# Expert bounds in registers and two gather buffers in an attention and mixture-of-experts kernel

## Chip, core and metric

The program runs on one core of one Trainium2 chip. The metric is the device time of one execution in microseconds (us). TensorE does the matmuls, VectorE, ScalarE and GpSimd the elementwise work; SyncE, ScalarE and GpSimd issue DMAs. Each engine has a sequencer of its own, which also does register arithmetic, branches and loads of values into registers.

## What is computed

A transformer block on x of 2 x 1024 tokens and 512 features: layer norm, causal attention with 16 heads in 4 groups, a shared two-layer MLP, and 32 experts of which each token uses 6. The part the change concerns:

```python
idx, w = _route(xf, Wr, br)                 # 6 of 32 experts a token
gate = jnp.zeros((T, E), w.dtype).at[jnp.arange(T)[:, None], idx].add(w)
def step(acc, ew):
    w1, w2, g = ew                          # 256 x 512 and 512 x 256
    h = jnp.square(jax.nn.relu(xf @ w1.T)) @ w2.T
    return (acc + g[:, None] * h, None)
acc, _ = jax.lax.scan(step, jnp.zeros_like(xf), (W1, W2, gate.T))
...
x = x + attention(xn) + shared(xn) + acc
```

## The kernel before

The kernel has three stages. The first (to about 190 us) normalises, routes, runs the shared MLP and builds a list of tokens sorted by expert, cut into tiles of 128 rows. The second (190 to 611 us) runs the experts over these tiles. The third does attention and adds the experts' rows, gathered by token, to the output.

Precision is kept by splitting every fp32 operand into an upper and a lower fp32r part, so each product is three matmuls (upper by upper, upper by lower, lower by upper).

**The expert stage.** The number of tiles of an expert depends on the data. `place_rows` on VectorE writes the first tile of each expert to `first_pair` in SBUF (`pairs` are tiles there); every expert has at least two. `pair_bound` (L355) loads one entry into a register of the engine that asks. `over_experts` loops over 8 rounds (`es`) of 4 experts (`s` in `SLOTS`, each with its own weight slot) and calls the engine's body with the bounds `lo` and `hi`. In `over_experts` of before, a round loads its first `lo`, and each expert loads its `hi`. Each body does tile `lo` outside of the inner loop, with the pieces of weight work of that expert around it, and the others in a loop over `lo + 1` to `hi`.

Five engines run the same loops side by side, tied by semaphores only:

- SyncE (`store_tiles`): for each expert it issues the load of the weights three experts ahead (`eraw <- we`, 1 MB, L442), then per tile the store of the tile's output rows (`expert_outputs <- ysb`, L451). The bounds of an expert are read before its weight load.
- GpSimd: one flat loop over all tiles. For tile p it waits until `mx_ready` tells that buffer p % XG is free, compares p % XG with each slot number, and in the slot that fits copies the tile's row numbers (L598), runs the small operation `settle` (L390), and starts the gather of 128 rows of normalised tokens into `xg[:, slot]` (L601, an indirect DMA, queue 0).
- TensorE (`expert_tiles`): `hidden_tile(p)` does 12 matmuls with the first weights (L800, L801, L804), and then, again by comparing (p + 1) % XG with each slot number (L807), `transpose_gathered` of the gathered rows of tile p + 1, four transposes (L792), after a wait for `xg_in` of that slot. They free the buffer: the last one adds to `mx_ready`. `output_tile(p - 1)` follows, six matmuls with the second weights (L815, L816, L819), then `transpose_hidden(p)`, two transposes (L828) that need `mhsq`.
- ScalarE (`expert_uppers`): per tile `mrelu`, `xgT_hi`, the copy of the output to `ysb`, and `hT_hi`; per expert four pieces of upper weight parts (L1086) two experts ahead.
- VectorE (`expert_lowers`): per tile `mhsq`, `xgT_lo`, `hT_lo`; per expert four pieces of lower weight parts (`w_lo`, L1210).

XG is 4, so a gather may start once the transposes of the tile four before are done. What is named `xg` holds 128 x 512 fp32 per buffer. The order of the work around the change is that in which the code is written; no planner moves it.

Of the kernel before, what the change touches and what calls it, by code (L numbers as in the profile page):

```python
# [8 lines left out]
I32 = mybir.dt.int32  # L9
# [4 lines left out]
P = 128  # L14
# [6 lines left out]
E, M = 32, 256  # L21
# [19 lines left out]
COMB = 3  # L41
MINT = T * TOPK // P
MAXT = MINT + 2 * E
XG = 4
YB = 4
WP = 4
NCOMB = TOPK * NT // GROUPS
# [68 lines left out]
def moe_attention_kernel(nc, x, wa, we, wr, br, out):  # L116
# [10 lines left out]
    with ExitStack() as ctx:  # L127
        def sb(name, shape, dt, stack=ctx):
            return stack.enter_context(nc.sbuf_tensor(name, shape, dt))
# [12 lines left out]
        y_rows = sb("y_rows", [P, TILES, 8], I32)  # L142
        y_gate = sb("y_gate", [P, TILES, TOPK], F32)
        tok_idx = sb("tok_idx", [P, MAXT + 1], I32)
        first_pair = sb("first_pair", [P, 2, E + 1], I32)
        comb_idx = sb("comb_idx", [P, NCOMB], I32)
        comb = sb("comb", [P, COMB, D], F32)
        araw = sb("araw", [P, 2, PIECE], F32)
# [204 lines left out]
        def pair_bound(eng, e, row=0):  # L353

            return eng.value_load(first_pair[0:1, row, bass.ds(e, 1)], min_val=0, max_val=MAXT + row)  # L355
# [14 lines left out]

            return slice(c * (W_COLS // WP), (c + 1) * (W_COLS // WP))

        def over_experts(eng, body, row=0):

            with eng.Fori(0, E // SLOTS) as es:
                lo = pair_bound(eng, es * SLOTS, row)
                for s in range(SLOTS):
                    hi = pair_bound(eng, es * SLOTS + s + 1, row)
                    body(es * SLOTS + s, s, lo, hi, es)
                    lo = hi  # L380

        def attend_groups(eng, attend, turn):
            attend(FIRST, turn * GROUPS)
# [11 lines left out]
        def _(sp):  # L395
# [43 lines left out]
            def store_tiles(e, s, lo, hi, es):  # L439

                sp.wait_ge(ew_lo, (e + (NSH + 2)) * WP)
                sp.dma_start(eraw[:, (s + AHEAD) % 2, :],  # L442
                             we[bass.ds((e + AHEAD) * P, P), :]).then_inc(eraw_in[(s + AHEAD) % 2], 16)
                with sp.Fori(lo, hi) as p:

                    for half in range(2):
                        with sp.If(p % 2 == half):
                            sp.wait_ge(y_stored[half], past((p // 2) * 16))
                            sp.sem_inc(y_free, 1)
                            sp.wait_ge(y_copied, past(p + 1))  # L450
                            sp.dma_start(y_d[bass.ds(p * P, P), :],  # L451
                                         ysb[:, bass.ds(p % YB, 1), :].rearrange("p s d -> p (s d)")
                                         ).then_inc(y_stored[half], 16)

            over_experts(sp, store_tiles)

# [174 lines left out]
        def _(pe):  # L631
# [163 lines left out]
            def hidden_tile(p, s):  # L795

                w_hi, w_lo = w1(hi_slot(s)), w1(lo_slot(s))
                pe.wait_ge(mx_hi, p + 1)
                for k in range(KD):
                    pe.matmul(ps_h, xgT_hi[:, k, :], w_hi[:, k, :], start=(k == 0), stop=False)  # L800
                    pe.matmul(ps_h, xgT_hi[:, k, :], w_lo[:, k, :], start=False, stop=False)  # L801
                pe.wait_ge(mx_lo, p + 1)
                for k in range(KD):
                    mm = pe.matmul(ps_h, xgT_lo[:, k, :], w_hi[:, k, :], start=False, stop=(k == KD - 1))  # L804
                mm.then_inc(mh_ready, 1)
                for slot in range(XG):
                    with pe.If((p + 1) % XG == slot):  # L807
                        transpose_gathered(slot, p + 1)
# [13 lines left out]
            def transpose_hidden(p, weights=None):  # L822
                pe.wait_ge(mhsq_ready, past(p + 1))
                for m in range(KM):
                    if m and weights is not None:

                        pe.wait_ge(ew_lo, weights)
                    mm = pe.transpose(ps_g[:, m * P:(m + 1) * P], mhsq[:, m * P:(m + 1) * P], ident[:, :])  # L828
                mm.then_inc(mt_ready, 1)
# [6 lines left out]
            def expert_tiles(e, s, lo, hi, es):  # L836

                pe.wait_ge(ew_lo, (e + NSH) * WP + 2)
                hidden_tile(lo, s)
                if s:  # L840
                    output_tile(lo - 1, s - 1)
                else:
                    with pe.If(es > 0):
                        output_tile(lo - 1, SLOTS - 1)
                transpose_hidden(lo, (e + (NSH + 1)) * WP)
                with pe.Fori(lo + 1, hi) as p:
                    hidden_tile(p, s)
                    output_tile(p - 1, s)
                    transpose_hidden(p)

            over_experts(pe, expert_tiles)
            output_tile(pair_bound(pe, E) - 1, SLOTS - 1)
# [104 lines left out]
        def _(act):  # L957
# [160 lines left out]
            def expert_uppers(e, s, lo, hi, es):  # L1118

                arrived, slot = e // 2 + (NSH // 2 + 2), (s + 2) % SLOTS  # L1120
                relu_hidden(lo)
                upper_tokens(lo + 1)
                upper_weights(0, slot, arrived)
                if s:
                    copy_output(lo - 1)
                else:
                    with act.If(es > 0):
                        copy_output(lo - 1)
                upper_hidden(lo)
                upper_weights(1, slot, arrived)  # L1130
                with act.Fori(lo + 1, hi) as p:
                    relu_hidden(p)
                    upper_tokens(p + 1)
                    copy_output(p - 1)
                    upper_hidden(p)
                upper_weights(2, slot, arrived)
                upper_weights(3, slot, arrived)

            over_experts(act, expert_uppers)
            copy_output(pair_bound(act, E) - 1)  # L1140
# [64 lines left out]
        def _(dve):  # L1205
# [112 lines left out]
            def place_rows():  # L1318

                dve.wait_ge(ranks_ready, 1)  # L1320
                for h in range(2):
                    dve.wait_ge(xn_out[h], 16 * B)
                dve.wait_ge(xnT_ready, B * NT)
                chain(dve.tensor_scalar(pairs_f, ps_total, float(P - 1), None, ALU.add))
                chain(dve.tensor_copy(pairs_i[:, :], pairs_f))
                chain(dve.tensor_scalar(pairs_i[:, :], pairs_i[:, :], 7, None, ALU.logical_shift_right))
                chain(dve.tensor_copy(pairs_f, pairs_i[:, :]))
                chain(dve.tensor_scalar(pairs_f, pairs_f, 2.0, None, ALU.max))
                chain(dve.tensor_tensor_scan(scan_f, scan_ones[:, :], pairs_f, 0.0, ALU.mult, ALU.add))
                chain(dve.memset(first_pair[:, :, 0:1], 0))  # L1330
                for row in range(2):
                    chain(dve.tensor_copy(first_pair[:, row, 1:E + 1], scan_f))
                dve.tensor_scalar(first_pair[:, 1, E:E + 1], scan_f[:, E - 1:E], 1.0, None, ALU.add).then_inc(pairs_ready, 1)
                dve.wait_ge(pairs_ready, 1)

                chain(dve.tensor_tensor(row_base, scan_f, pairs_f, ALU.subtract))
                chain(dve.tensor_scalar(row_base, row_base, float(P), 1.0, ALU.mult, ALU.add))
                chain(dve.tensor_tensor(rrow, ps_rank[:, :].rearrange("p (t e) -> p t e", t=TILES),
                                        row_base.unsqueeze(1).to_broadcast([P, TILES, E]), ALU.add))
                chain(dve.tensor_tensor(rrow, rrow, rsel[:, :, :].bitcast(F32), ALU.mult))  # L1340
                hold()
                for t in range(TILES):
                    last = dve.max(out=top_y[:, t, :], in_=rrow[:, t, :])
                chain(last)
                dve.tensor_scalar(y_rows[:, :, :], top_y[:, :, :], -1.0, None, ALU.add).then_inc(y_rows_ready, 1)
                dve.wait_ge(y_rows_ready, 1)
                chain(dve.tensor_scalar(part_i[:, 0, :, :], y_rows[:, :, :], P - 1, None, ALU.bitwise_and))
                chain(dve.tensor_scalar(part_i[:, 1, :, :], y_rows[:, :, :], 7, None, ALU.logical_shift_right))
                chain(dve.tensor_copy(part_f[:, :, :, :], part_i[:, :, :, :]))
# [111 lines left out]
            def expert_lowers(e, s, lo, hi, es):  # L1461
                slot = (s + 2) % SLOTS
                square_hidden(lo)
                lower_tokens(lo + 1)
                lower_weights(e + 2, 0, slot)
                lower_hidden(lo)
                lower_weights(e + 2, 1, slot)
                with dve.Fori(lo + 1, hi) as p:
                    square_hidden(p)
                    lower_tokens(p + 1)  # L1470
                    lower_hidden(p)
                lower_weights(e + 2, 2, slot)
                lower_weights(e + 2, 3, slot)

            over_experts(dve, expert_lowers)

# [111 lines left out]
```

## Time and profile before

| | us |
|---|---|
| median of 3 runs (1704.72 to 1709.8) | 1704.78 |
| the profiled execution | 1705.53 |
| its span, first to last instruction | 1703.8 |
| of the span: first stage with the change over to the experts | 206 |
| expert stage from its third tile on, 206 to 611 | 405 |
| attention and the rest | 1093 |

The span is what the profile's views divide up; the profiled execution is 1.7 us longer than it. Busy TensorE in the views means that its pipeline holds a matmul, and a granted clock of 1.00 is 2.4 GHz, 0.50 is 1.2 GHz. Register, branch and load-to-register instructions are not counted as busy; they show under the queue of their engine (PEldq, DVEq, ACTq, SPq) in the view of a source line. "issue" as a releaser is idle time that ends with nothing the profile shows.

### The profile page before, as it was taken

Reading aid. Unit: us, or ns where it says so; the run is one execution under the profiler, and the core shown is the slowest. Engines: PE = TensorE matmul, PEld = TensorE weight load, DVE = VectorE, ACT = ScalarE, POOL = GpSimd, SP = SyncE. Lnnn points to the kernel's source line nnn. Section 1 sums busy time; section 2 is a strip of 40 time slices with the busy share of each in tenths; the row PEclk is TensorE's granted clock in tenths of the full one; section 3 lists DMA queues with packets and bytes.
Section 4 is the critical chain, followed back from the end, with each engine's and each line's share of the span. In section 5 each row is a group of like instructions: output and inputs, shape, how many; then the busy total and the mean of one; then the engine's idle time right before and its main releaser. Section 6 shows DMA issues by size and latency. Waiting matters only on the chain.

```text
span 1703.8 us, 31632 instructions
## 1 busy us (share of the span) xinstructions
PE 1580.1 (93%) x8812; PEld 1349.1 (79%) x8813; DVE 1174.4 (69%) x2277; ACT 823.0 (48%) x1687; POOL 355.6 (21%) x590
## 2 busy tenths in 40 slices
PE   6886899999999969999999999995999999999996
PEld 5765688888888857888888888874788888888885
DVE  5679665565666545866866876872795785785785
ACT  3410266666666643544544544542454453453453
POOL 3541433333333310011011011020101101101101
PEclk9988799999999989999999999997999999999999
DMA  5850466666676640111111110214101201201102
GB/s 199 315 229 1 136 215 217 226 217 222 209 234 212 218 160 32 32 56 51 31 55 50 31 55 25 93 45 143 44 20 56 62 19 56 62 19 56 38 7 81
DMA packets 61736, 180.15 MB, mean 106 GB/s; under 512 B 6736, under 2 KB 6864, under 8 KB 56912
## 3 DMA queue, kind: packets, MB, share of 16 engines
q1 hardware_dynamic: 36800, 107.84, 18.3%
q0 software_dynamic: 16640, 54.54, 11.5%
q10 hardware_dynamic: 8208, 16.78, 2.6%
q8 instruction: 34, 0.56, 0.1%
q14 instruction: 54, 0.44, 0.1%
HBM read 122.77 MB, written 56.36 MB: 105 GB/s over the span
## 4 chain that ended last, share of the span: by engine, by line
PE 86%; DVE 7%; issue 3%; ACT 1%; DMA 1%; DVEq 0%; ACTq 0%; POOLq 0%; SPq 0%
PE bank L638 8%; PE bank L640 8%; PE bank L639 8%; PE bank L919 7%; PE ps_s L638 5%; PE ps_s L640 5%; PE ps_s L639 5%; PE ps_s L907 4%; PE ps_s L902 4%; PE ps_s L908 4%; PE ps_s L800 4%; PE ps_s L804 3%; PE ps_s L801 3%; PE ps_s L815 3%; PE ps_s L819 3%
## 5 line engine op out<-in xcount | busy, mean ns | idle before, releaser
L1180 ACT ACTIVATE probs<-ps_s,negmax 128x128 f32<-128x128 f32 (+7 forms) x256 | 189.6, 741 | 187.2 <-DVE negmax L1506 186.1
L1210 DVE TENSOR_TENSOR pT_lo<-bank,pT_hi 128x512 fp32r<-128x512 f32 x288 | 196.5, 687 | 76.4 <-ACT pT_hi L1188 75.0
L1188 ACT ACTIVATE pT_hi<-bank 128x512 fp32r<-128x512 f32 x288 | 169.1, 597 | 149.7 <-PE bank L919 148.4
L390 POOL TENSOR_TENSOR settled<-ident 128x1 f32<-128x1 f32 x192 | 54.7, 285 | 774.1 <-DVE acc L1533 764.4
L1506 DVE TENSOR_REDUCE negmax<-ps_s 128x1 f32<-128x128 f32 (+7 forms) x256 | 189.2, 751 | 21.6 <-issue 9.8
L638 PE MATMUL ps_s<-xT_hi,wa_hi 128*128 128x512 f32 x384 | 156.3, 407 | 26.5 <-DVE wa_lo L1210 26.5
L919 PE MATMUL bank<-ident,probs 128*128 128x128 f32 x1152 | 167.4, 272 | 2.0 <-DVE pT_lo L1210 2.0
L919 PEld LDWEIGHTS bank<-ident,probs 128*128 128x128 f32 x1152 | 139.5, 141 | 29.8 <-DVE pT_lo L1210 2.4
L640 PE MATMUL ps_s<-xT_hi,wa_lo 128*128 128x512 f32 x384 | 153.1, 399 | 0.0
L639 PE MATMUL ps_s<-xT_lo,wa_hi 128*128 128x512 f32 x384 | 152.5, 397 | 0.0
L902 PE MATMUL ps_s<-kT_hi,qT_hi 128*128 128x512 f32 (+3 forms) x384 | 140.2, 365 | 8.3 <-ACT probs L1180 5.4
L907 PE MATMUL ps_s<-kT_lo,qT_hi 128*128 128x512 f32 (+3 forms) x384 | 142.4, 371 | 0.0
L800 PE MATMUL ps_s<-w_hi,xgT_hi 128*128 128x256 f32 x444 | 121.8, 307 | 21.7 <-issue 16.6
L1513 DVE TENSOR_SCALAR probs<-probs,rnorm 128x128 f32<-128x128 f32 (+7 forms) x256 | 133.3, 521 | 9.1
L908 PE MATMUL ps_s<-kT_hi,qT_lo 128*128 128x512 f32 (+3 forms) x384 | 132.8, 346 | 0.0
L638 PE MATMUL bank<-pT_hi,v_hi 128*128 128x512 f32 x288 | 125.0, 434 | 3.1 <-DVE cT_lo L1210 3.1
L601 POOL DMA_INDIRECT xg<-normed_tokens,comb_idx x112 | 115.7, 1033 | 24.1 <-issue 20.4
L1210 DVE TENSOR_TENSOR hT_lo<-ps_s,hT_hi 128x256 fp32r<-128x256 f32 x111 | 47.1, 424 | 96.9 <-ACT hT_hi L1096 66.8
L640 PE MATMUL bank<-pT_hi,v_lo 128*128 128x512 f32 x288 | 113.6, 394 | 0.0
L639 PE MATMUL bank<-pT_lo,v_hi 128*128 128x512 f32 x288 | 112.8, 392 | 0.0
L801 PE MATMUL ps_s<-w_lo,xgT_hi 128*128 128x256 f32 x444 | 111.9, 284 | 0.0
L800 PEld LDWEIGHTS ps_s<-w_hi,xgT_hi 128*128 128x128 f32 x444 | 84.9, 191 | 30.2 <-issue 29.3
(188 smaller groups left out, 3740.1 us busy)
## 6 DMA issues: line engine op xcount, KB each, us to landing
eraw<-we SPq DMA_DIRECT2D x37, 1024.0 KB
expert_outputs<-ysb SPq DMA_DIRECT2D x111, 256.0 KB
araw<-wa SPq DMA_DIRECT2D x40, 512.0 KB, 3.9
expert_outputs<-comb ACTq DMA_DIRECT2D x1, 16384.0 KB, 52.5
normed_tokens<-xn SPq DMA_DIRECT2D x4, 1024.0 KB, 6.7
out<-acc SPq DMA_DIRECT2D x2, 2048.0 KB, 7.8
res<-x SPq DMA_DIRECT2D x2, 1024.0 KB, 6.6
acc<-x SPq DMA_DIRECT2D x2, 1024.0 KB, 14.0
```

The source lines that it names most:

```text
L638: pe.matmul(out_, lh, rh, start=(first and k == 0), stop=False)
L639: pe.matmul(out_, lh, rl, start=False, stop=False)
L640: mm = pe.matmul(out_, ll, rh, start=False, stop=(last and k == parts - 1))
L800: pe.matmul(ps_h, xgT_hi[:, k, :], w_hi[:, k, :], start=(k == 0), stop=False)
L902: pe.matmul(o, q_h, kT_hi[:, ks], start=True, stop=False)
L907: pe.matmul(o, q_h, kT_lo[:, ks], start=False, stop=False)
L908: mm = pe.matmul(o, q_l, kT_hi[:, ks], start=False, stop=True)
L919: mm = pe.transpose(ps_t[blk % 2][:, h * P:(h + 1) * P], probs[:, i % 2, h, a * P:(a + 1) * P], ident[:, :])
L1180: act.activation(probs[:, i % 2, a, 0:keys], src, ACT.Exp, bias=negmax[:, i % 2, a:a + 1], accum_out=rowsum[:, i % 2, a:a + 1]).then_inc(e ...
L1188: act.activation(pT_hi[:, blk % RING, :], ps_t[blk % 2][:, :], ACT.Copy).then_inc(pt_hi_ready, 1)
L1210: dve.tensor_tensor(out_, whole, upper.bitcast(F32), ALU.subtract).then_inc(signal, 1)
L1506: dve.tensor_reduce(negmax[:, i % 2, a:a + 1], src, AX.X, ALU.max, negate=True).then_inc(max_ready, 1)
```

## The change

It has three parts. In `over_experts` the first bounds are set before the loop (0, and a load of entry 1), and both are kept in two registers from round to round. Each body now loads the bound of the expert after the next one (`after = pair_bound(..., e + 2)`) at a place of its own and returns it: SyncE behind the weight load, TensorE behind `hidden_tile(lo)`, ScalarE behind `upper_hidden(lo)`, VectorE behind `lower_hidden(lo)`. XG goes from 4 to 2, in the buffers, their semaphores and the comparisons of TensorE and GpSimd. `first_pair` gets one more entry, which is cleared with the others since the last expert's load reads it. The number and the work of the tiles stay.

```diff
-XG = 4
+XG = 2
...
-        first_pair = sb("first_pair", [P, 2, E + 1], I32)
+        first_pair = sb("first_pair", [P, 2, E + 2], I32)
...
-        def over_experts(eng, body, row=0):
+        def over_experts(eng, body):
+            lo_reg = eng.alloc_register()
+            hi_reg = eng.alloc_register()
+            eng.reg_mov(lo_reg, 0)
+            eng.reg_mov(hi_reg, pair_bound(eng, 1))
             with eng.Fori(0, E // SLOTS) as es:
-                lo = pair_bound(eng, es * SLOTS, row)
+                lo = eng.snap(lo_reg, min_val=0, max_val=MAXT)
+                hi = eng.snap(hi_reg, min_val=0, max_val=MAXT)
                 for s in range(SLOTS):
-                    hi = pair_bound(eng, es * SLOTS + s + 1, row)
-                    body(es * SLOTS + s, s, lo, hi, es)
-                    lo = hi
+                    lo, hi = hi, body(es * SLOTS + s, s, lo, hi, es)
+                eng.reg_mov(lo_reg, lo)
+                eng.reg_mov(hi_reg, hi)
...
                              we[bass.ds((e + AHEAD) * P, P), :]).then_inc(eraw_in[(s + AHEAD) % 2], 16)
+                after = pair_bound(sp, e + 2)
                 with sp.Fori(lo, hi) as p:
...
                 hidden_tile(lo, s)
+                after = pair_bound(pe, e + 2)
                 if s:
                     output_tile(lo - 1, s - 1)
...
                 upper_hidden(lo)
+                after = pair_bound(act, e + 2)
                 upper_weights(1, slot, arrived)
...
-                chain(dve.memset(first_pair[:, :, 0:1], 0))
+                chain(dve.memset(first_pair[:, :, :], 0))
...
                 lower_hidden(lo)
+                after = pair_bound(dve, e + 2)
                 lower_weights(e + 2, 1, slot)
```

On TensorE, where one expert ends and the next begins, before: L828 is `transpose_hidden` of the last tile, L846 the inner loop's end, L800 the first matmul of `hidden_tile(lo)`.

```order
L828 MATMUL ps_s<-ident,mhsq 128x128 [waits mhsq_ready]
L828 MATMUL ps_s<-ident,mhsq 128x128
L846 REGISTER_ALU
L846 COMPARE_AND_BRANCH
L355 REGISTER_ALU
L355 TENSOR_LOAD first_pair
L355 ISA x2
L838 REGISTER_ALU
L798 REGISTER_ALU [waits ew_lo]
L800 MATMUL ps_s<-w_hi,xgT_hi 128x256 [waits mx_hi]
```

The same place after (L835, L854 and L807 are the lines just named):

```order
L835 MATMUL ps_s<-ident,mhsq 128x128 [waits mhsq_ready]
L835 MATMUL ps_s<-ident,mhsq 128x128
L854 REGISTER_ALU
L854 COMPARE_AND_BRANCH
L845 REGISTER_ALU
L805 REGISTER_ALU [waits ew_lo]
L807 MATMUL ps_s<-w_hi,xgT_hi 128x256 [waits mx_hi]
```

The load is gone from there. After, it stands in the middle of an expert's first tile, behind the second and last of the slot comparisons (L814) with its transposes (L799) and in front of `output_tile` (L822):

```order
L814 COMPARE_AND_BRANCH
L797 ISA
L799 MATMUL ps_s<-ident,xg 128x128 [waits xg_in1]
L799 MATMUL ps_s<-ident,xg 128x128 x3
L814 UNCONDITIONAL_BRANCH
L355 REGISTER_ALU
L355 TENSOR_LOAD first_pair
L355 ISA x2
L851 COMPARE_AND_BRANCH
L822 MATMUL ps_s<-w_hi,hT_hi 128x512 [waits mhhi_ready]
```

So the load moved behind the wait for `xg_in`, and two of four comparisons are gone. On VectorE, in the first tile of an expert after the change (L1221 is the subtraction that L1210 was, L1451 the square that L1440 was):

```order
L1221 TENSOR_TENSOR hT_lo<-ps_s,hT_hi 128x256 [waits mhhi_ready]
L355 ISA
L355 TENSOR_LOAD first_pair
L355 ISA x2
L1459 REGISTER_ALU
L1221 TENSOR_TENSOR w_lo<-eraw,w_hi 128x512 [waits ew_hi]
L1480 ISA
L1480 UNCONDITIONAL_BRANCH
L1480 ISA
L1451 TENSOR_TENSOR mhsq<-mrelu 128x256 [waits mrelu_ready]
```

Before, VectorE had its load between the last piece of an expert's `w_lo` and the square of the next expert's first tile; now it is between `hT_lo` of the first tile and the second piece of `w_lo`.

## Rows read from the trace of the kernel before

**Rows 1.** The page, first line.

```profile
span 1703.8 us, 31632 instructions
```

**Rows 2.** Windows (start:end length, busy us by engine, clock, DMA share, GB/s).

```profile
190.00:206.00 16.00, 10.50 (x51) 9.35 (x50) 12.93 (x20) 7.02 (x15) 5.15 (x8) 0.68 0.55 204
206.00:611.00 405.00, 387.14 (x2600) 344.07 (x2599) 242.04 (x449) 264.67 (x558) 151.81 (x316) 1.00 0.69 218
```

**Rows 3.** Timeline of TensorE (start us, us, engine line, operation, idle before).

```profile
205.25 0.36 PE L800 MATMUL ps_s<-w_hi,xgT_hi 128*128 128x256 f32 x1
...
248.56 0.36 PE L800 MATMUL ps_s<-w_hi,xgT_hi 128*128 128x256 f32 x1
...
253.62 0.38 PE L800 MATMUL ps_s<-w_hi,xgT_hi 128*128 128x256 f32 x1 [1.33 <-issue]
...
257.11 0.36 PE L800 MATMUL ps_s<-w_hi,xgT_hi 128*128 128x256 f32 x1
...
264.07 0.36 PE L800 MATMUL ps_s<-w_hi,xgT_hi 128*128 128x256 f32 x1
...
267.85 0.38 PE L800 MATMUL ps_s<-w_hi,xgT_hi 128*128 128x256 f32 x1
...
269.38 0.60 PE L792 MATMUL ps_s<-ident,xg 128*128 128x128 f32 x4
...
279.78 0.38 PE L800 MATMUL ps_s<-w_hi,xgT_hi 128*128 128x256 f32 x1 [0.75 <-issue]
...
609.50 0.36 PE L800 MATMUL ps_s<-w_hi,xgT_hi 128*128 128x256 f32 x1
```

**Rows 4.** Waits, 206 to 611 us (us in total, times, longest).

```profile
POOL comb_idx L598 <- PE ps_s L792: 210.6, 105, 3.7
...
PEld ps_s L800 <- issue: 24.6, 31, 1.8
...
PEld ps_s L828 <- DVE mhsq L1440: 2.4, 9, 0.4
```

**Rows 5.** Source line L355 (count, ns min/median/max, first and last start).

```profile
L355 PEldq FUSED_REGOPS  x49: 51/157/171, 188.4 to 613.2; - x49
L355 PEldq TENSOR_LOAD <-first_pair x41: 299/337/1119, 187.9 to 612.6; - x41
...
L355 DVEq TENSOR_LOAD <-first_pair x40: 305/486/1003, 196.4 to 604.2; - x40
```

**Rows 6.** Source line L807, the slot comparisons of TensorE.

```profile
L807 PEldq COMPARE_BRANCH  x444: 66/200/373, 195.5 to 610.5; - x148
```

**Rows 7.** Timeline of VectorE, mhsq of an expert's second and third tile.

```profile
552.66 0.42 DVE L1440 TENSOR_TENSOR mhsq<-mrelu 128x256 f32<-128x256 f32 x1
...
556.02 0.42 DVE L1440 TENSOR_TENSOR mhsq<-mrelu 128x256 f32<-128x256 f32 x1 [0.60 <-ACT mrelu L1092]
```

**Rows 8.** Timeline of SyncE's queue, three of 32 weight loads.

```profile
274.43 0.36 SPq L442 DMA_DIRECT2D eraw<-we  x1
...
374.02 0.36 SPq L442 DMA_DIRECT2D eraw<-we  x1
...
500.50 0.36 SPq L442 DMA_DIRECT2D eraw<-we  x1
```

**Rows 9.** Timeline of GpSimd, two of 112 gathers.

```profile
270.99 0.99 POOL L601 DMA_INDIRECT xg<-normed_tokens,comb_idx  x1 [0.21 <-issue]
...
275.11 0.99 POOL L601 DMA_INDIRECT xg<-normed_tokens,comb_idx  x1 [0.23 <-issue]
```

**Rows 10.** Gather queue, packets in windows 256.88:260.28, 374.59:379.79, 500.80:506.40.

```profile
q0 software_dynamic: 80, 0.26, 31.0%
...
q0 software_dynamic: 73, 0.22, 10.8%
...
q0 software_dynamic: 80, 0.26, 12.7%
```

**Rows 11.** The queue of weights and stores, window 300.96:304.43 (packets, MB, share).

```profile
q1 hardware_dynamic: 203, 1.00, 88.2%
```

More of the change, by code:

```diff
@@ L453, in store_tiles @@
                                          ).then_inc(y_stored[half], 16)
+                return after
             over_experts(sp, store_tiles)
@@ L849, in expert_tiles @@
                     transpose_hidden(p)
+                return after
             over_experts(pe, expert_tiles)
@@ L1137, in expert_uppers @@
                 upper_weights(3, slot, arrived)
+                return after
             over_experts(act, expert_uppers)
@@ L1473, in expert_lowers @@
                 lower_weights(e + 2, 3, slot)
+                return after
             over_experts(dve, expert_lowers)
```

## Prediction, made before the changed kernel ran

> **What bounds the kernel now.** The windows by stage come first [rows 1, 2]. The change touches the expert stage, 206 to 611 us: there TensorE is busy 387 of 405 us at the full clock (1.00), so TensorE's stream of tiles sets the time, and the stages around it stay as they are. TensorE's own timeline shows the pace: two tiles take 6.96 us inside an expert (257.11 to 264.07), 3.48 each, but 3.78 us pass before the tile at 267.85, which opens an expert, and 5.06 us pass before the one at 253.62 (248.56 to 253.62), which also opens a round of four experts [rows 3]. There are 111 tiles (444 comparisons, four each [rows 6]). From the third, 205.25, to the last, 609.50, there are 108 periods, 404.25 us; at 3.48 they would be 375.8. So **28.4 us** are lost at the openings of experts. The waits put 24.6 us of idle before the weights of L800 down to "issue", nothing the profile shows as a releaser [rows 4]. The source view of L355 tells what it is: TENSOR_LOAD of a bound on TensorE's queue, 299/337/1119 ns, followed by register work (157 ns) [rows 5]. One is in front of every expert, two in front of a round.
>
> **Loads of bounds on TensorE.** A load with its register work takes 0.31 + 0.16 us and the steps between, about 0.75 us (a round's second load costs 5.06 - 3.78 = 1.28 us together with the loop's own branch). Inside an expert the sequencer has 0.3 to 0.4 us in hand, so an ordinary border loses 0.3 us, more when the load is slow (up to 1.1), and a round 1.6. After the change nothing of this stands between transpose_hidden of the last tile and hidden_tile of the next. Ordinary borders (24) should show no gap at all; at the 7 rounds the two register moves and the loop's branch remain, and I leave 0.3 us each, 2 us. Of the 28.4 some 3 us are not in front of L800 but in the middle of a tile, before L828 (2.4 us at waits for mhsq [rows 4]): VectorE's own load sits before square_hidden(lo) and makes mhsq late. **Removed: 28.4 - 3 - 2 = 23 us.** Bounds: 20 and 26.
>
> **The same loads in their new places.** TensorE: the sequencer reaches the load about 0.9 us after the tile's start (it is held until xgT_lo is there, then passes two comparisons of 0.2 us [rows 6]), is through at 1.65, and output_tile's first weights are due at 1.87. Hidden, cover 0.2 us, as long as nothing holds the sequencer before it. VectorE: the load follows lower_hidden(lo) and precedes weight piece 1. Now mhsq of an expert's second tile starts 552.66, right behind that piece; undisturbed it would come 3.48 before the next one, 556.02, so at 552.54 [rows 7]. With at least 0.31 us of load and as much register work as TensorE's, the piece and mhsq come about 0.35 later still, 0.45 in all, and TensorE bears 0.35 (the hand of the sequencer above): some 0.1 us an expert, 3 us, and the 3 us of today's late mhsq go. Zero net; bounds -3 and +8 (VectorE's load has a median of 486 ns [rows 5]). ScalarE: its load stands behind upper_hidden(lo) while copy_output still runs on the engine, and its queue is served in order behind that; nothing, bound 2 us. SyncE: the weight load eraw leaves before the bound is read, so some 0.7 us earlier by the same sum (274.43 [rows 8] would be 273.7); the store behind it waits for ysb anyway. A page of the Trainium skill (DMA: Bandwidth & Descriptors, section Latency and other measured facts) gives tensor_load a floor of about 600 ns. The rows show 299 on TensorE, so here the floor does not hold; by it VectorE's piece would come 0.3 us later in 32 experts and the sum would rise by up to 9 us.
>
> **Four comparisons to two.** TensorE's cost 200 ns each [rows 6] but run while matmuls stream; worth nothing in steady state. On GpSimd the gather of slot 0 leaves 3.14 us after its tile's start (270.99 against 267.85) [rows 3, 9], each further slot one comparison later, near 0.15; slots 2 and 3 vanish. Nothing on the path by itself.
>
> **Two gather buffers instead of four** is the expensive part. GpSimd waits for TensorE's transposes in every tile already (210.6 us, 105 times [rows 4]): it fills a buffer the moment it is free. The gather for tile p may start when the transposes of p - 4 are done; now of p - 2. Those stand in tile p - 3, the gather leaves 3.14 to 3.3 us into that tile, and its rows are read by L792 some 1.5 us into tile p - 1 (269.38 against 267.85 [rows 3]). The time it has is 2 x 3.48 + 1.5 - 3.2 = **5.2 us**, where it had 12.2. How long does it take? The one issued at 256.88, with no weight load near, had its 80 packets by 3.4 us [rows 10]. Gathers issued within a microsecond behind a weight load are slow: that of 374.59, 0.57 us behind the load of 374.02, had 73 of 80 by 5.2 us; that of 500.80, 0.3 us behind, had all 80 only by 5.6 [rows 8, 10]. The weight load and its neighbours keep the DMA engines 88% busy and move 1.00 MB in 3.5 us [rows 11]; a gather behind all of it would need 3.4 + 3.5 = 6.9. So one gather in each expert (31 of them) overruns: by 0.3 us at the low end, by 1.7 at the high end, and I take 1.1 for the pattern of today. The earlier eraw shifts the pair apart by 0.7 us, of which I credit 0.2: 0.9 x 31 = **28 us**.
>
> **The new place of the load makes that worse.** The weight load leaves 6.6 us after its expert's first tile began (274.43 less 267.85 [rows 3, 8]), after the change near 5.9 or less, in the second tile; the gather it hits is the second tile's (275.11 [rows 9]), which after the change is for three tiles on, so that its transposes stand in the fourth tile. In an expert of three tiles (267.85 to 279.78 [rows 3]; I count 19 of 32 experts that way) the fourth is the next expert's first, where the bound is loaded right behind the transposes. TensorE's sequencer is then held at xg_in, and comparison plus load (0.2 + 0.75 us) start only when the rows land, against 0.44 us of transposes (four at 0.11) that cover them: 0.45 us on top, 19 x 0.45 = **8.5 us**.
>
> **Sum.** -23 + 0 + 28 + 8.5 = +13.5. Span 1703.8 + 13.5 = 1717.3; the profiled execution took 1705.5, 1.7 more than its span, and the median of the runs is 1704.78, 0.75 below it: 1718.3 for a median. **Forecast 1718 us**, slower.
>
> **Rivals.** (1) *Turn-taking hides the gather.* If DMA engines alternate between the gather's queue and the weights' queue, a gather's four 4 KB packets an engine (64 of its 80, over 16) wait for four weight packets at most, 8 of which an engine moves in 3.5 us, 0.43 each: 3.4 + 1.7 = 5.1 us, just within 5.2. Then no transposes wait, only the 23 us count, and the time is 1682, 1 to 8 us more with stragglers. That is the other side, and it decides at 5.2 us. Against it stand the 73 of 80 packets at exactly that point, and the 80 of 500.80 only at 5.6. The Trainium skill has the rule (DMA: Bandwidth & Descriptors, section Queues, rings and completion order): each engine round-robins between its queues, packet by packet. By that rule, these traces disagree. (2) *Balance.* With eraw 0.7 us earlier and the gather up to 0.3 earlier, the second may meet only the tail of the first. At 0.5 us an overrun, 15 us, and 5 for the loads behind: 1702, no difference. For it: 500.80, 0.3 us behind its weight load, overran by only 0.4. Against: 374.59 and 275.11 sit 0.57 and 0.68 us behind theirs, and that is where most sit today. (3) *Worse.* Overruns at 1.7 and 0.5 more in the short experts, 62 us less 23, to 1744; and long pauses can cost the clock: it stood at 0.68 in 190 to 206, where TensorE was busy 10.5 of 16 us, while the gaps of up to 1.8 us in the expert stage never moved it from 1.00 [rows 2, 4]. Stalls of 2 to 3 us lie between. (4) *The registers do not hold the bounds* and the loads stay: nothing supports it, the order shows the loads moved.
>
> **Chances.** Forecast with its spread (1708 to 1733) 0.64; balance (1700 to 1710) 0.15; turn-taking and anything else under 1700, 0.12; worse than 1733, 0.09. The likeliest case gives the time. To hold 8 in 10 the range takes the forecast's spread and the balance: 1701 to 1733. About 0.3% (5 us) is what a measurement of this kernel can tell from no change: faster 0.12, same 0.16, slower 0.72.
>
> **What the profile after would show.** Right: no idle "issue" over 0.1 us before the first expert matmul at ordinary borders; TENSOR_LOAD on TensorE mostly near 300 ns, since it no longer falls 3 to 4 us behind eraw; a new wait of TensorE's transposes for the DMA of xg, about one an expert, near 1 us, 25 to 40 us in all; more idle before output_tile in first tiles of experts than elsewhere; GpSimd's wait for ps_s unchanged in kind. Wrong: if the waits for xg sum to less than 15 us, the overruns are mis-sized; if output_tile waits for nothing in first tiles, the last 8.5 us are wrong; if TensorE pauses before L828 in second tiles by more than 0.2 us, VectorE's load was underrated; if the granted clock drops below 1.00 in the expert stage, the third rival holds.

## The result, and the profile after

| | before | after |
|---|---|---|
| median of 4 runs each, us | 1705.9 | 1731.08 (1728.39 to 1737.47) |
| span of the profiled execution | 1703.8 | 1728.0 |
| third tile to last tile on TensorE, 108 periods | 404.25 | 428.51 |

The changed kernel takes 1.0146 of the time before (95% interval 1.0121 to 1.017): 25 us slower, where 13 were forecast. All of it lies in the expert stage, as the last row shows. Of the kernels below, the one with SyncE alone changed had one execution of four at a granted clock of 0.58 (2528.93 us), which is left out of its median. The page, the windows (as [rows 2]; the third is one of five short stretches at half clock) and TensorE's timeline (as [rows 3]):

```profile
span 1728.0 us, 31078 instructions
```

```profile
190.00:206.00 16.00, 10.48 (x49) 9.19 (x48) 13.06 (x20) 7.05 (x14) 3.61 (x7) 0.68 0.53 205
206.00:637.00 431.00, 398.44 (x2611) 351.93 (x2610) 238.77 (x451) 261.43 (x560) 156.19 (x322) 0.98 0.64 207
350.50:353.90 3.40, 3.40 (x16) 3.10 (x15) 1.75 (x4) 1.51 (x4) 0.99 (x1) 0.50 0.39 124
```

```profile
205.43 0.38 PE L807 MATMUL ps_s<-w_hi,xgT_hi 128*128 128x256 f32 x1
...
309.65 0.38 PE L807 MATMUL ps_s<-w_hi,xgT_hi 128*128 128x256 f32 x1
...
310.70 0.64 PE L811 MATMUL ps_s<-w_hi,xgT_lo 128*128 128x256 f32 x4
313.16 0.66 PE L799 MATMUL ps_s<-ident,xg 128*128 128x128 f32 x4 [1.82 <-DMA xg<-normed_tokens,comb_idx]
314.31 0.49 PE L822 MATMUL ps_s<-w_hi,hT_hi 128*128 128x512 f32 x1 [0.49 <-issue]
...
315.93 0.36 PE L807 MATMUL ps_s<-w_hi,xgT_hi 128*128 128x256 f32 x1
...
633.94 0.37 PE L807 MATMUL ps_s<-w_hi,xgT_hi 128*128 128x256 f32 x1
```

The tile at 309.65 opens an expert and takes 6.28 us instead of 3.48. Its border is clean, but the transposes (L799) wait 1.82 us for the gathered rows, and then output_tile (L822) waits another 0.49 us, because TensorE's sequencer had been held at the same wait and reached the bound load only afterwards. The waits of after, 206 to 637 us (as [rows 4]), and the loads of bounds (as [rows 5]):

```profile
POOL comb_idx L605 <- PE ps_s L799: 238.5, 107, 4.2
...
PEld ps_s L799 <- DMA xg<-normed_tokens,comb_idx: 31.7, 21, 2.3
...
PEld ps_s L822 <- issue: 8.8, 16, 1.0
...
PEld ps_s L835 <- DVE mhsq L1451: 3.0, 13, 0.2
...
PEld ps_s L807 <- issue: 0.2, 1, 0.2
```

```profile
L355 PEldq TENSOR_LOAD <-first_pair x34: 298/303/671, 187.8 to 637.0; - x34
...
L355 DVEq TENSOR_LOAD <-first_pair x33: 300/306/548, 196.3 to 631.7; - x33
```

The 24.6 us of "issue" before an expert's first matmul [rows 4] are down to 0.2. GpSimd's wait for the transposes is of the kind it was (238.5 us against 210.6). New is a wait of 31.7 us for `xg`, 21 times. (PEld is TensorE's loading of weights, where its idle time is counted.) SyncE's and GpSimd's queues show how a gather comes late:

```profile
304.38 0.35 SPq L447 DMA_DIRECT2D eraw<-we  x1
```

```profile
302.43 0.99 POOL L608 DMA_INDIRECT xg<-normed_tokens,comb_idx  x1
...
305.88 1.00 POOL L608 DMA_INDIRECT xg<-normed_tokens,comb_idx  x1
...
309.37 0.99 POOL L608 DMA_INDIRECT xg<-normed_tokens,comb_idx  x1 [0.24 <-issue]
```

and the gather queue q0 in the 3.4 us behind each of the first two gathers, 302.43:305.83 and 305.88:309.28, for the second with the queue of weights and stores q1 (packets, MB, share):

```profile
q0 software_dynamic: 79, 0.26, 36.7%
...
q1 hardware_dynamic: 181, 0.92, 81.7%
q0 software_dynamic: 5, 0.02, 13.8%
```

The gather 1.95 us ahead of the weight load has 79 packets done in 3.4 us. The one 1.50 us behind it has 5, and the transposes that read it start at 313.16, 7.3 us after its issue, where 5.2 were to be had. It is the rule and not one border: of the 28 gathers that leave less than 1.8 us behind a weight load, 25 start at most 19 of their 80 packets in 3.4 us.

The view of the chain that ended last (window 300 to 330) runs through this gather:

```profile
305.04 0.42 POOL comb_idx L605
...
305.88 7.24 DMA xg<-normed_tokens,comb_idx
313.16 0.66 PE ps_s L799 x4
313.82 0.49 issue
```

**Where the 24 us are.** I split each of the 108 periods of TensorE's timeline at its four steps (first matmul, L799, L822, L835) and took off the undisturbed 3.48 us:

| us over the stage | before | after |
|---|---|---|
| ahead of an expert's or tile's first matmul | 26.5 | 3.9 |
| ahead of the transposes, for xg | 0.4 | 31.0 |
| ahead of output_tile | -0.2 | 10.3 |
| late mhsq | 1.4 | 0.15 |
| matmuls at half clock, five stretches of 3.4 us | 0 | 7.0 |
| sum | 28.1 | 52.3 |

The half-clock row is an estimate: each such stretch lengthens the work in it by about 1.4 us, not by the half of 3.4, since part of it is idle or loads. The row of late mhsq counts what the tile's period lost, and the wait row of L835 above (3.0 us) counts idle of PEld; most of that idle lengthens no period.

### The profile page after: what moved, and what is told of

Same layout as the page of the kernel before. It is cut to its first block, busy times and chain, and to the rows that moved or that the text cites. A ratio compares the mean times of both kernels' runs of the same rounds, so it can differ in the third digit from the quotient of the medians.

```text
span 1728.0 us, 31078 instructions
## 1 busy us (share of the span) xinstructions
PE 1590.2 (92%) x8812; PEld 1356.7 (79%) x8813; DVE 1169.8 (68%) x2277; ACT 819.0 (47%) x1687; POOL 353.1 (20%) x590
## 4 chain that ended last, share of the span: by engine, by line
PE 78%; DMA 9%; DVE 7%; issue 3%; ACT 1%; POOL 1%; POOLq 0%; SPq 0%; DVEq 0%; ACTq 0%
PE bank L645 8%; PE bank L647 8%; PE bank L646 8%; DMA xg<-normed_tokens,comb_idx 8%; PE bank L928 7%; PE ps_s L645 5%; PE ps_s L647 5%; PE ps_s L646 5%; PE ps_s L916 4%; PE ps_s L911 4%; PE ps_s L917 4%; PE ps_s L799 3%; PE ps_s L807 2%; PE ps_s L822 2%; PE ps_s L808 2%
## 5 line engine op out<-in xcount | busy, mean ns | idle before, releaser
L1221 DVE TENSOR_TENSOR pT_lo<-bank,pT_hi 128x512 fp32r<-128x512 f32 x288 | 196.3, 686 | 77.2 <-ACT pT_hi L1199 75.8
L807 PE MATMUL ps_s<-w_hi,xgT_hi 128*128 128x256 f32 x444 | 123.9, 310 | 4.2 <-DVE w_lo L1221 4.2
L1221 DVE TENSOR_TENSOR hT_lo<-ps_s,hT_hi 128x256 fp32r<-128x256 f32 x111 | 47.1, 425 | 108.6 <-ACT hT_hi L1105 107.1
L1111 ACT ACTIVATE ysb<-ps_s 128x512 f32 x111 | 66.4, 599 | 99.0 <-PE ps_s L826 91.2
```

The lines of the kernel that those rows point to most:

```text
L1221: dve.tensor_tensor(out_, whole, upper.bitcast(F32), ALU.subtract).then_inc(signal, 1)
```

## Experiments

All kernels were timed against the kernel before on the same chip. "After" is the changed kernel. Each time is the median; behind it stands the ratio to the kernel before with its 95% interval. Waits are PEld rows for 206 to 637 us unless said; falls of the clock are those of the profiled execution.

**The two parts apart.** First the bounds in registers with four buffers:

```diff
-XG = 2
+XG = 4
```

> The changed kernel with four gather buffers, so that only the bounds differ from the kernel before. Theory (two buffers cost, moved loads gain): the 22.6 us of gaps at the openings of experts and 1.3 us of late mhsq stay away, and with 12.2 us of window no gather is waited for: 1705.9 - 24 = 1682 us, granted clock 1.00 through the expert stage, no wait of the transposes for xg. Rival (the loads in their new places cost about what they free, and the slower time has its source there): 1700 us or more, with the waits before output_tile still near 10 us.

Measured: 1685.75 us, 0.9889 [0.9872, 0.9905]; no wait for xg, no fall of the clock in the stage. The 4 us over my 1682 are mostly waits before output_tile, 3.6 us. Then two buffers in the kernel before, with its loads at the borders:

```diff
-XG = 4
+XG = 2
```

> The kernel before with two gather buffers and two comparisons, bounds loaded as before. Theory: the gaps at the openings stay (26 us) and widen the window of the gathers that span them, so the waits for xg are somewhat shorter than after the change, 20 to 30 us in all, with no extra 10 us behind them in first tiles, and 0 to 7 us from drops of the clock: 1706 + 27 = 1733, between 1726 and 1742. Rival (moved loads are the cause): 1706, no change.

Measured: 1722.02 us, 1.0106 [1.0089, 1.0123]. Its waits:

```profile
PEld ps_s L800 <- issue: 21.9, 26, 2.1
PEld ps_s L792 <- DMA xg<-normed_tokens,comb_idx: 16.2, 18, 3.0
```

That is less than the 1726 to 1742 that I expected, as the waits for xg are 16 us and not 20 to 30, and the clock fell once. The bounds alone bring 20 us and the buffers alone cost 16. Together that would be a gain of 3; the change as a whole lost 25. **Twenty-nine us come from the two parts meeting** (26 by the ratios, some 6 either way), and the next runs are about those.

**Is it the weight load?** After, with a weight load that brings an eighth of the columns and leaves out the other seven:

```diff
-                sp.dma_start(eraw[:, (s + AHEAD) % 2, :],
-                             we[bass.ds((e + AHEAD) * P, P), :])
+                sp.dma_start(eraw[:, (s + AHEAD) % 2, 0:W_COLS // 8],
+                             we[bass.ds((e + AHEAD) * P, P), 0:W_COLS // 8])
```

> The changed kernel, in which SyncE's weight load of an expert brings only an eighth of its columns (256 columns of the 2048 of each row, 128 KB instead of 1 MB); seven eighths of the weights of the experts are not loaded. Theory (a gather is late only where its packets share the DMA engines with a weight load, which makes it 5.6 to 8.3 us instead of 3.3 to 4.0): no wait for xg of more than 1 us in all, no clock drop in the expert stage, and 1731 - 31 (waits for xg) - 7 (clock) - 3 to 10 (the pauses before output_tile, which go if only a stall exposes the load) = 1680 to 1690 us. Rival (two buffers are simply too few: GpSimd learns too late that a buffer is free, whatever the DMA queues do): the waits stay near 30 us and the time over 1715.

Measured: 1683.18 us, 0.9867 [0.9851, 0.9883]. No row for xg among the waits, no fall of the clock. The gather at 297.42, 1.49 us behind its weight load (295.93), as the late one above, in 297.42:300.82:

```profile
q0 software_dynamic: 80, 0.26, 29.8%
```

All 80 packets. The gathers stand to the weight loads nearly as after (medians of 2.15 us ahead and 1.4 behind, against 2.5 and 1.3), so it is not their place alone but what they meet there. Two buffers are enough where a gather meets 128 KB; the 1 MB beside it makes it late, and without it the stalls, the pauses behind them and the falls of the clock are gone together.

**Where the weight load falls.** In the kernel before, one or two loads of bounds and the loop stood on SyncE between the last store of an expert and the next weight load; after, the weight load leaves first. I moved it back by one bound load, which I took for half of the way:

```diff
+                after = pair_bound(sp, e + 2)
                 sp.wait_ge(ew_lo, (e + (NSH + 2)) * WP)
                 sp.dma_start(eraw[:, (s + AHEAD) % 2, :], ...
-                after = pair_bound(sp, e + 2)
```

> The changed kernel with SyncE's bound load moved from behind the weight load to ahead of it, which issues the weight load 0.5 us later, as half of the way back to where the kernel before had it (two loads and more of loop ahead of it, 1.25 us in all). Theory of the place in time (after the change the weight load falls 2 us behind one gather and 1.2 us ahead of the next, so that both share its time): waits for xg fall from 31 us to about 24, and the time to about 1722 us. Rival (the waits are a matter of TensorE's faster borders, not of where the weight load falls): no change, 1728 to 1734 us.

Measured: 1724.69 us, 1.0112 [1.0095, 1.0129]:

```profile
PEld ps_s L799 <- DMA xg<-normed_tokens,comb_idx: 21.9, 27, 2.2
...
PEld ps_s L822 <- issue: 15.0, 19, 1.1
```

Then four loads ahead of it:

```diff
+                after = pair_bound(sp, e + 2)
+                for _ in range(3):
+                    pair_bound(sp, e + 2)
                 sp.wait_ge(ew_lo, (e + (NSH + 2)) * WP)
```

> The same with four bound loads on SyncE ahead of the weight load (three of them again the same one), which issue it some 2 us later than in the changed kernel. Theory of the place in time: the gather before the weight load has nearly landed, the next is issued 0.8 us ahead of it instead of 1.2 us behind: waits for xg at or below the 16 us of the old kernel with two buffers, the time 1700 to 1712 us. Rival (faster borders): 1728 to 1734 us. If the late gather is only moved from one tile to the next, also 1728 or more.

Measured: 1716.64 us, 1.0065 [1.0046, 1.0085]:

```profile
PEld ps_s L801 <- DMA xg<-normed_tokens,comb_idx: 27.0, 20, 2.1
...
PEld ps_s L824 <- issue: 4.5, 10, 0.8
```

The first run came out as the theory of the place says, the second only in its sign. (By its median place, 0.6 us ahead of the next gather, the first one went the whole way back, not half.) The time of the second is above my 1700 to 1712, and its waits for xg don't fall to 16. The gather that I expected 0.8 us ahead of the weight load stands 1.6 ahead, and the next 1.9 behind (medians of 31): the weight load has moved past one gather into the path of the next. 16 of the 20 waits now lie in an expert's later tiles and not in its first. With that, half of the pauses before output_tile are gone (the load of the bound is not behind those waits) and all falls of the clock, and the late gather stays. The counter-test makes SyncE alone early, in the kernel before with two buffers:

```diff
-XG = 4
+XG = 2
...
-            over_experts(sp, store_tiles)
+                return after
+
+            over_experts_ahead(sp, store_tiles)
```

> The kernel before with two gather buffers, and with the new handling of bounds on SyncE alone; the other engines load theirs at the borders as before. Its weight load comes about 1.2 us sooner against the gathers than in the kernel before with two buffers (1722.0 us), while TensorE's borders stay slow. Theory of the place in time: waits for xg rise from 16 to 25 us or more, the time to 1730 to 1738 us. Rival (faster borders make the difference): still 1720 to 1724 us.

Measured: 1731.82 us (median of three), 1.0165 [1.0139, 1.019]:

```profile
PEld ps_s L809 <- DMA xg<-normed_tokens,comb_idx: 28.8, 28, 2.6
...
PEld ps_s L817 <- issue: 17.6, 25, 1.5
```

Weight load and gathers around one border of it, SyncE's queue and then GpSimd's:

```profile
308.15 0.35 SPq L456 DMA_DIRECT2D eraw<-we  x1
```

```profile
306.08 1.00 POOL L618 DMA_INDIRECT xg<-normed_tokens,comb_idx  x1
309.35 1.00 POOL L618 DMA_INDIRECT xg<-normed_tokens,comb_idx  x1
```

and the same two views of the kernel with two buffers and SyncE's old order:

```profile
303.93 0.36 SPq L442 DMA_DIRECT2D eraw<-we  x1
```

```profile
301.25 1.00 POOL L601 DMA_INDIRECT xg<-normed_tokens,comb_idx  x1
304.88 0.99 POOL L601 DMA_INDIRECT xg<-normed_tokens,comb_idx  x1 [0.24 <-issue]
```

With SyncE early a gather is 2.1 us ahead of the weight load and the next 1.2 behind. In the old order they were 2.7 ahead and 0.95 behind. Over all 31 weight loads the median for the one behind is 1.2 with SyncE early, 1.3 in after, and 0.5 in the old order and 0.6 in the run with one load ahead. These 0.7 us of place cost 10 us (1731.82 against 1722.02), about a third of the 29; the clock fell twice there and once in the old order, so some 1.4 of the 10 may be its.

Why the early place is worse can be counted from the packets of the traces. I took, from 206 to 600 us of eight kernels (before, after, the runs with whole weights up to here, and the one with three buffers), the weight loads with a gather less than 1.8 us behind them. Where the gather ahead had left 3.3 us or more before the weight load (36 times), the load's last packet ended 4.9 us after its issue (4.5 to 5.4), and the gather behind had its 80 packets after 5.3 (medians). Where the gather ahead had left only 1.5 to 2.6 us before (98 times), the load took 7.0 us (5.3 to 7.6) and the gather behind 6.0. Of this late kind are 16 weight loads in after, 20 with SyncE alone, 2 in the run with one load ahead, and none in the old order with two buffers. A gather still under way thus goes with a late load and a late next gather; that the one makes the other late is my inference.

**The load behind the wait.** After, with TensorE's bound load behind output_tile:

```diff
                 hidden_tile(lo, s)
-                after = pair_bound(pe, e + 2)
                 if s:
                     output_tile(lo - 1, s - 1)
...
+                after = pair_bound(pe, e + 2)
                 transpose_hidden(lo, (e + (NSH + 1)) * WP)
```

> The changed kernel with TensorE's load of the next bound moved from in front of output_tile in an expert's first tile to behind it. Theory (the load queued behind the wait for gathered rows costs 10 us of its own): the waits before output_tile in first tiles fall from 9.8 us to under 2, those for xg stay near 31: 1731 - 9 = 1722, down to 1718 if shorter pauses also save some of the five drops of the clock. Rival (that idle is part of the gathers' lateness, wherever the load stands): 1731, no change.

Measured: 1730.08 us, 1.0141 [1.0107, 1.0174], no gain that can be told from after (the third to the last tile take 429.40 us against 428.51). The row before L822 is gone; the other one has grown:

```profile
PEld ps_s L799 <- DMA xg<-normed_tokens,comb_idx: 42.1, 29, 2.6
```

After, the two rows were 31.7 + 8.8 = 40.5; now they are 42.1 + 0. The pause was time that TensorE would have spent waiting for a later gather. The same is seen at the borders: the SyncE-alone kernel has 17.6 us of them and 1731.82 us, after has next to none and 1731.08. With two buffers and an early weight load the chain gather, transposes, next gather sets the time, and TensorE's own savings are paid back as longer waits. This is the rest of the 29 us: with four buffers the new bounds bring 20 us, and here, from the SyncE-alone kernel to after, 0.7. With the 10 of the place that makes 29 (and in it lie the falls of the clock, five in after and two with SyncE alone). The pages say the same of the chain that ended last, before and after:

```profile
PE 86%; DVE 7%; issue 3%; ACT 1%; DMA 1%; DVEq 0%; ACTq 0%; POOLq 0%; SPq 0%
```

```profile
PE 78%; DMA 9%; DVE 7%; issue 3%; ACT 1%; POOL 1%; POOLq 0%; SPq 0%; DVEq 0%; ACTq 0%
```

DMAs have 12% of it with SyncE alone and with TensorE's load moved, and 1% again with an eighth of the weights and with a third buffer, which comes next.

**A third buffer.**

```diff
-XG = 2
+XG = 3
```

> The changed kernel with three gather buffers and three comparisons. The window grows from 5.2 to 8.7 us, and the slowest gather of the traces took about 8. Theory (it is a threshold of time): all of it goes, 1682 to 1684 us, as with four. Rival (fewer buffers cost in proportion): about half way, 1705 us.

Measured: 1681.17 us, 0.9858 [0.9842, 0.9874], the fastest kernel of the study. It was run once more:

> The changed kernel with three gather buffers once more, in more rounds and beside its variant with VectorE's load moved: 1680 to 1683 us as in its first measurement (1681.2 us), 0.984 to 0.988 of the time before.

Measured: 1682.6 us, 0.9862 [0.9846, 0.9877]. Its waits in the stage:

```profile
PEld ps_s L835 <- DVE mhsq L1451: 5.8, 25, 0.2
...
PEld ps_s L822 <- issue: 0.2, 1, 0.2
```

No wait for xg. The kernel with four buffers had 3.6 us, 16 times, before L822. Split by periods, as in the table above, output_tile comes late by 6.0 us with four and by 0.9 with three. One comparison less may be what lets the load finish in time; with three buffers and the old bounds it brings nothing:

> The kernel before with three gather buffers and three comparisons a tile, and nothing else. With the new bounds, three buffers were 4.5 us faster than four, and the pause before output_tile fell from 3.6 to 0.2 us. If that is TensorE's sequencer, which has less to do ahead of a tile by one comparison, it helps the old borders as well, where the sequencer is late too: 0.1 us or so at each of 31 borders, 1701 to 1704 us. If the gain needs the load in its new place, 1705 to 1707 us.

Measured: 1705.4 us, 0.9997 [0.9987, 1.0006].

**Whose loads cost the time?** The kernel before, with TensorE alone on the new bounds:

```diff
-            over_experts(pe, expert_tiles)
+                return after
+
+            over_experts_ahead(pe, expert_tiles)
```

> The kernel before with its four gather buffers, and with the new handling of bounds on TensorE alone; the other engines load theirs at the borders as before. If TensorE's own loads are the whole cost of the borders (26.5 us of them in the expert stage of before, of which the kernel with the new bounds on all engines keeps 2.2), the time comes to 1683 to 1688 us. If the other engines' loads bring the next inputs late to TensorE (VectorE's squares above all, 0.2 to 0.6 us a border), 5 to 15 us of it stay as waits: 1690 to 1700 us.

Measured: 1703.51 us, 0.9981 [0.9972, 0.999], 2.6 us instead of 20, less than either guess. Its waits (206 to 610), a border in VectorE's timeline and in that of TensorE's weight loads, and VectorE's loads of bounds:

```profile
PEld ps_s L842 <- DVE mhsq L1456: 21.8, 31, 1.3
...
PEld ps_s L829 <- issue: 4.3, 20, 0.4
```

```profile
270.23 1.30 DVE L1226 TENSOR_TENSOR w_lo<-eraw,w_hi 128x512 fp32r<-128x512 f32 x2
272.09 0.42 DVE L1456 TENSOR_TENSOR mhsq<-mrelu 128x256 f32<-128x256 f32 x1 [0.56 <-issue]
```

```profile
272.57 0.23 PEld L842 LDWEIGHTS ps_s<-ident,mhsq 128*128 128x128 f32 x2 [0.69 <-DVE mhsq L1456]
```

```profile
L355 DVEq TENSOR_LOAD <-first_pair x40: 308/562/920, 197.0 to 603.2; - x40
```

VectorE does two pieces of weights, then its own load, then the squares; TensorE, no longer late itself, now waits for these squares at all 31 borders. Two engines' loads cost much the same time side by side, and the first one hid the second. No run changed VectorE, ScalarE or SyncE alone with four buffers, so how the other 17 us divide among them is not measured. It goes the other way too, with VectorE's load alone moved behind its loop (three buffers):

```diff
                 lower_hidden(lo)
-                after = pair_bound(dve, e + 2)
                 lower_weights(e + 2, 1, slot)
...
                     lower_hidden(p)
+                after = pair_bound(dve, e + 2)
                 lower_weights(e + 2, 2, slot)
```

> The changed kernel with three gather buffers, and with VectorE's bound load moved from ahead of the second piece of weights to behind the loop over the expert's tiles. With three buffers, TensorE waits 25 times 0.2 us for the squares of the second tile of an expert, which VectorE makes late after its load and a piece of weights. If the load is what makes them late, 3 to 5 us go: 1677 to 1679 us. If the piece of weights is, nothing changes, or the load's 0.5 us makes the next expert's first squares late: 1681 to 1684 us.

Measured: 1695.55 us, 0.9932 [0.9918, 0.9946]: 13 us slower than with the load in its place (1682.6), where I allowed 3.

```profile
PEld ps_s L835 <- DVE mhsq L1451: 20.0, 31, 0.7
```

VectorE has nothing in hand at the border: half a microsecond there is paid by TensorE 31 times (13 / 31 = 0.42 us).

## Why the prediction was right and wrong

The direction and the mechanism were right: two buffers leave a gather 5.2 us, one behind a weight load misses that, and the loss is larger than what the bounds give back. **The step that failed is the size of what the late gathers cost.** The prediction had +28 for them and +8.5 for the load behind the wait, 36.5 us, and put the clock at nothing. The trace shows 31.0 + 10.3 = 41.3 us, and by estimate 7.0 more at half clock. The measured time still lies near the upper end of the 1708 to 1733 that the forecast gave itself.

**Loads at the borders, -23.** Right in size as rows: 28.1 became 3.9 + 0.15, so -24.0, and the run with four buffers gained 19.8 us with everything counted. But it priced TensorE's queue alone and put VectorE's part at 3 us. VectorE's was about as long and only hidden behind TensorE's; the sum held because the change moves both. And as a saving of time it did not add to the other terms: with two buffers and an early weight load it brought 0.7 us, the rest came back as waits for xg.

**Loads in their new places, 0.** Nearly right. With four buffers output_tile comes late by 3.6 us of waits (6.0 in the split), just past the 0.2 us of cover. VectorE's later mhsq was to cost TensorE 3 us; the waits are there (3.0 us, 13 times, at most 0.2), but the split has 0.15 us for them. TensorE's loads are near 300 ns (303), as forecast. The Trainium skill gives 600 ns as a floor (DMA: Bandwidth & Descriptors, Latency and other measured facts); it does not hold here on TensorE or VectorE, whose minima after are 298 and 300 ns.

**Two buffers, +28.** The kind was right and so was the sum, nearly: 31.0. Its parts were not. The pattern of the kernel before was worth 16, not 1.1 x 31 = 34. And the term's correction, "The earlier eraw shifts the pair apart by 0.7 us, of which I credit 0.2", has the wrong sign. The same shift brings the weight load closer to the gather ahead, and where it stands near, the load itself is late (7.0 us instead of 4.9 to its last packet), and so is the gather behind. The runs price the shift at +10. That 28 came so near is luck: 34 was too much, and the correction went the wrong way.

**The load behind the wait, +8.5.** As a row it was right (8.8 us in 16 pauses, 10.3 in my split), as a term of a sum wrong: without it the time is the same. Two waits on the same chain don't add.

**What the sum lacked: the clock.** It fell to 0.50 five times for 3.4 us, some 7 us in all. The prediction had this in its third rival and gave it no term in the forecast, although a stall of 2 us was in its own upper bound (1.7 us, with 0.45 behind it).

So the sum of 13.5 was short by 10.8, in rows of the trace: the clock +7.0, gathers +3.0, the load +1.8, borders and mhsq -1.0. Of the rivals, turn-taking (1) in its turns of single 4 KB packets is refuted by the 5 packets, and balance (2) by the waits of 31.7 us; what came is the forecast's mechanism with the third rival's clock.

## What to carry over

A wait that appears in place of another is only priced by asking which chain then binds: savings off that chain are worth nothing, as the load moved behind output_tile was (0 of 8.8 us) and the faster borders were (0.7 of 20). A shift of 0.7 us in when a large DMA leaves can be worth more (10 us) than the instructions one counts. When several engines carry the same overhead at a border, look at each queue: removing it on one (2.6 us) shows the next, on all (20 us) it pays. Before cutting buffers, put the time to spare beside the slowest transfer in the new order, and try one buffer more than the least: three here were 4.6 us faster than four.

## What the runs showed of the hardware

A 256 KB gather behind a 1 MB load is not slowed in proportion but nearly stopped at first: 5 packets in 3.4 us against 79 or 80, while the queue of weights and stores moved 181 packets and 0.92 MB. The Trainium skill has engines take turns between their queues packet by packet (DMA: Bandwidth & Descriptors, Queues, rings and completion order). An even turn of the packets that the trace counts, of 4 KB for the gather and 8 KB for the weights, would not give 5 against 181. But the section's packet is a bundle of typically 9 to 17 descriptors. The prediction read it as one of the trace's packets and called the traces in disagreement. If one packet of the trace is one descriptor, an engine's whole share of the weight load, 128 / 16 = 8, fits into a single packet of the skill's, and a gather behind it would wait for all of it: then the rule and these windows agree. No view tells which holds. With a gather under way the weight load itself is late too (7.0 us instead of 4.9, counted above); why, the runs don't tell.

The granted clock can fall behind a single pause. This is the row ahead of the half-clock stretch at 350.5; TensorE was idle for 2.03 us and had worked again for 1.8 us when the clock went from 1.00 (2.4 GHz) to 0.50 (1.2 GHz):

```profile
348.69 0.65 PE L799 MATMUL ps_s<-ident,xg 128*128 128x128 f32 x4 [2.03 <-DMA xg<-normed_tokens,comb_idx]
```

The length of the pause alone does not decide. In the same trace a pause of 2.13 us that ended at 434.2 had no fall behind it, while the fall at 377.8 came behind pauses of 1.20 and 0.37 us; with four loads ahead of the weight load there were six pauses of 1.5 to 1.9 us and no fall.

A load of a bound took 303 ns in the median on TensorE after, and 306 on VectorE where the change puts it. On VectorE at the border it took 562 in the median and up to 920 with TensorE alone changed (before, 486 and 1003 [rows 5]). What slows it there no run isolates.
